# A four-layer gated cross-attention kernel: one batch's rows normalised ahead of the other's, and weight turns placed anew

## The reference, cut to what matters

```python
# second layer, feed-forward (quantised, with a Hadamard transform)
gate = bitlinear(x, w_gate); up = bitlinear(x, w_up)          # 256 -> 1024, rows rounded to 8 bits
intermediate = jax.nn.silu(gate) * up
return h_bitlinear(intermediate, w_down)                      # fwht over 1024, round to 8 bits, 1024 -> 256

# third layer: the attention branch is a mixing of rows with a learned adjacency
return (1.0 - gamma) * adj_raw + gamma * A_learned            # adj_raw is the normalised x
# third layer, feed-forward: a shared part and two of eight experts
g = x @ sw1.T; u = x @ sw2.T
shared_out = jax.nn.silu(g) * u @ sw3.T                       # 256 -> 1024 -> 256
scores = jax.nn.sigmoid(x @ router_w.T)
_, top_idx = jax.lax.top_k(scores + expert_bias, TOPK)
```

## Time and profile before

| what | value |
|---|---|
| median of 3 runs | 748.82 us (748.71 to 749.53) |
| profiled execution, its own time | 750.36 us |
| span of that execution | 748.5 us |
| PE busy | 663.1 us (89%) |
| DVE busy | 529.6 us (71%) |
| ACT busy | 350.4 us (47%) |
| POOL busy | 224.5 us (30%) |
| granted TensorE clock, mean | 0.972 |

### The profile page before, as it was taken

One profiled execution on the slowest core, in us unless ns is written; L12 is line 12 of the kernel. 1 busy time (PEld: TensorE's weight loads), 2 busy tenths in 40 slices (PEclk: granted clock), 3 DMA queues, 4 the chain that ended last, 5 costly groups with the idle time before them and its releaser, 6 DMA issues. The chain is left out here.

```text
span 748.5 us, 13940 instructions
## 1 busy us (share of the span) xinstructions
PE 663.1 (89%) x4446; PEld 455.1 (61%) x4446; DVE 529.6 (71%) x1617; ACT 350.4 (47%) x620; POOL 224.5 (30%) x315
## 2 busy tenths in 40 slices
PE   9998898898888887899789999976788989999997
PEld 4644476766764665487567778652233328777776
DVE  5686988879787788878875572757986967335545
ACT  2573456576455755142126326235488794122220
POOL 1000377812000122112315652632352220623430
PEclk9999999999999999999999999996799999999999
DMA  6997431050000230000071260012000053233315
GB/s 174 341 235 152 162 101 49 17 171 1 3 2 1 77 94 1 1 0 1 30 253 59 64 205 22 29 44 72 2 2 2 4 173 61 79 106 100 93 57 175
DMA packets 55565, 60.23 MB, mean 80 GB/s; under 512 B 13847, under 2 KB 48808, under 8 KB 55496
## 3 DMA queue, kind: packets, MB, share of 16 engines
q1 hardware_dynamic: 50408, 46.02, 21.8%
q0 software_dynamic: 4848, 13.28, 5.1%
q10 hardware_dynamic: 240, 0.05, 0.0%
HBM read 34.92 MB, written 24.20 MB: 79 GB/s over the span
## 5 line engine op out<-in xcount | busy, mean ns | idle before, releaser
L2068 ACT ACTIVATE arenas<-psum 128x512 f32<-128x512 f32 (+6 forms) x89 | 62.9, 733 | 47.9 <-PE psum L1215 40.0
L3356 DVE TENSOR_REDUCE arenas<-psum 128x2 f32<-128x512 f32 x96 | 61.8, 683 | 12.2 <-PE psum L1819 10.9
L1023 POOL TENSOR_SCALAR arenas<-arenas,small 128x1024 f32<-128x1024 f32 x8 | 9.0, 1124 | 151.3 <-DVE small L3047 151.3
L1040 POOL DMA_INDIRECT experts_l<-shared,small x30 | 29.5, 982 | 62.7 <-ACT shared L2381 51.7
L2068 ACT ACTIVATE late<-psum 128x512 f32<-128x512 f32 (+1 forms) x51 | 25.6, 503 | 43.1 <-PE psum L1215 43.0
L1215 PE MATMUL psum<-conb,shared 128*128 128x128 bf16 (+2 forms) x512 | 37.6, 229 | 7.2 <-issue 2.1
L1215 PEld LDWEIGHTS psum<-conb,shared 128*128 128x128 bf16 (+2 forms) x512 | 33.2, 118 | 14.6 <-issue 12.0
L1215 PE MATMUL psum<-con,early 128*128 128x128 f32 (+1 forms) x188 | 32.2, 282 | 10.7 <-ACT late L2068 5.1
L2428 ACT ACTIVATE early<-psum 128x1024 f32<-128x1024 f32 x32 | 32.0, 1031 | 17.1 <-PE psum L1836 16.7
L1703 PE MATMUL psum<-arenas,early 128*128 128x256 f32 x160 | 36.7, 383 | 1.1 <-DVE arenas L3510 1.1
L1703 PE MATMUL psum<-early,late 128*128 128x256 f32 x128 | 32.5, 403 | 5.4 <-DVE early L3249 5.3
(11 more groups left out here) (456 smaller groups left out, 1763.7 us busy)
## 6 DMA issues: line engine op xcount, KB each, us to landing
sorted_l<-late SPq DMA_DIRECT2D x3, 1920.0 KB, 17.4
early<-sorted_l SPq DMA_DIRECT2D x6, 645.0 KB, 5.8
early<-in_L_ffn_sw SPq DMA_DIRECT2D x3, 1024.0 KB, 9.7
late<-sorted_l SPq DMA_DIRECT2D x23, 129.0 KB, 2.1
sorted_l<-late SPq DMA_DIRECT2D x1, 2944.0 KB, 24.5
early<-in_L_ffn_We_gate_up SPq DMA_DIRECT2D x2, 1408.0 KB
early<-in_L_ffn_expert_w SPq DMA_DIRECT2D x2, 1024.0 KB, 6.8
early<-in_L_ffn_w SPq DMA_DIRECT2D x1, 2048.0 KB, 8.3
```

The lines of the kernel that those rows point to most:

```text
L1023: pool.tensor_scalar(ha[s][:, rows], ha[s][:, rows], c2[s][:, t:t + 1], ROUND, ALU.mult, ALU.add)
L1040: pool.indirect_dma_start(expert_rows2[p], bass.IndirectOffsetOnAxis(dest2[p][:, i:i + 1], 0), out_r2[k], None).then_inc(outs_sent[k], 16)
L2068: act.activation(dst, view(v), ACT.Copy, scale=scale).then_inc(f.drained(i, key), 1)
L3356: dve.tensor_reduce(nm, q3d(f.slot(0, ("max", w, k)), 2, S), X, ALU.max, negate=True)\
```

## The change

Four things are altered.

1. `beside_f1`: the same 25 turns of `prep2` stand at other steps. They stand one after the other, without gaps, from the turn of a product to the first parts of the transform, and none stands in the transform's third and fourth part.
2. `second_rows` in `ffn1`: statistics run ahead of the first multiplication, and the other seven parts behind the multiplications of the first two tiles instead of the first four.
3. `mix(0)` becomes `mix_first`: statistics and root of all four row tiles of the pair come first; batch 0's rows are written and signalled in the second step, before batch 1 is mixed; then batch 1 gets statistics and root anew and is written.
4. TensorE and ScalarE in `ffn2(0)`: eight constant matmuls, the turn of batch 0, the first two shared blocks of batch 0 (`AHEAD2`) with their silu, 14 constant matmuls, the turn of batch 1. Both turns now use bank 2, and the shared blocks keep banks 0 and 1.

```diff
--- before.py
+++ after.py
@@ -610,7 +610,9 @@
                         H=(h, 1, [("hT", i) for i in range(TILES2)]), D=(d, 1, [("dn", i) for i in range(TILES2)]))
 
         plan("l1f", 1, B=([4, 5], 1, products1(1)))
-        plan("l2f", 0, **ffn2_keys([0, 1], 2, [("AT", 0), ("AT", 1)]))
+        plan("l2f", 0, A=([2], 1, [("xT", 0), ("xT", 1), ("gate",), ("rank",)]),
+             B=([0, 1], 1, streams([("sh", j) for j in range(HC)]) + [("AT", 0), ("AT", 1)]), N=([2], 1, [("dn", 0), ("dn", 1)]))
+        AHEAD2 = 2
 
 
 
@@ -716,7 +718,7 @@
 
         THERE_F1 = 50
 
-        beside_f1 = paced(6, (22, 1.5)) + [41, 45, 48]
+        beside_f1 = [6, 7, 8, 9, 10, 11, 15, 16, 17, 18, 22, 23, 24, 25, 26, 27, 31, 32, 33, 34, 35, 36, 40, 41, 44]
 
         TILES_THERE = 9
 
@@ -1715,21 +1717,31 @@
 
                 fa, fb = pl["l2f"]["A"], pl["l2f"]["B"]
 
+                rows = (fa, fa if i == 0 else fb)
+
+                def shared2(s, j):
+                    shared_up(fb, i, s, j, xnT2[i], P, j * P, j * P, sw1T, sw2T, H_FFN)
+
                 if i == 0:
                     yield from steps(MIX)
-                if i == 0:
-                    kept_busy(fa, i, ("xT", 0), 34)
+                    kept_busy(fa, i, ("xT", 0), 8)
                 for s in range(2):
                     pe.wait_ge(xn_ready["l2f"].sem, xn_ready["l2f"].count(2 * i + s))
-                    turn((fa, fb)[s], i, ("xT", s), [(P, c * S + t * P, rows2[i][:, s * T + t, c * P:(c + 1) * P])
-                                                     for c in range(DC) for t in range(T)], ident)
+                    turn(rows[s], i, ("xT", s), [(P, c * S + t * P, rows2[i][:, s * T + t, c * P:(c + 1) * P])
+                                                 for c in range(DC) for t in range(T)], ident)
+                    if (i, s) == (0, 0):
+                        pe.wait_ge(fa.drained(0, ("xT", 0)), fa.read(0, ("xT", 0)))
+                        for j in range(AHEAD2):
+                            shared2(0, j)
+                        kept_busy(fa, i, ("xT", 1), 14)
                 yield
                 for s in range(2):
-                    pair_logits(fa, (fa, fb)[s], i, s, xnT2[i], r2T)
+                    pair_logits(fa, rows[s], i, s, xnT2[i], r2T)
                     yield
                 for s in range(2):
                     for j in range(HC):
-                        shared_up(fb, i, s, j, xnT2[i], P, j * P, j * P, sw1T, sw2T, H_FFN)
+                        if (i, s) != (0, 0) or j >= AHEAD2:
+                            shared2(s, j)
                         if (s, j) == RANK[i]:
                             pe.wait_ge(picks2_ready, i + 1)
                             rank(fa, i, 2 * T, picked2[i])
@@ -2338,10 +2350,19 @@
 
             def ffn2(i):
                 fa, fb = pl["l2f"]["A"], pl["l2f"]["B"]
+
+                def gate2(s, j):
+                    act.wait_ge(fb.filled, fb.full(i, ("sh", s, j)))
+                    v = fb.slot(i, ("sh", s, j))
+                    act.activation(sg2[i][fb.place(i, ("sh", s, j))], v[:, 0:S], ACT.Silu).then_inc(sg2_ready, 1)
+
                 if i == 0:
                     yield from steps(MIX)
                 for s in range(2):
-                    move((fa, fb)[s], i, ("xT", s), xnT2[i][s], lambda v: v[:, 0:W])
+                    move(fa if i == 0 else (fa, fb)[s], i, ("xT", s), xnT2[i][s], lambda v: v[:, 0:W])
+                    if (i, s) == (0, 0):
+                        for j in range(AHEAD2):
+                            gate2(0, j)
                 yield
                 yield
                 act.wait_ge(fa.filled, fa.full(i, ("gate",)))
@@ -2350,9 +2371,8 @@
                 yield
                 for s in range(2):
                     for j in range(HC):
-                        act.wait_ge(fb.filled, fb.full(i, ("sh", s, j)))
-                        v = fb.slot(i, ("sh", s, j))
-                        act.activation(sg2[i][fb.place(i, ("sh", s, j))], v[:, 0:S], ACT.Silu).then_inc(sg2_ready, 1)
+                        if (i, s) != (0, 0) or j >= AHEAD2:
+                            gate2(s, j)
                         yield
 
             def downs2(i):
@@ -3050,6 +3070,7 @@
 
                 alone(quantise(0))
                 second = second_rows()
+                advance(second, 1)
                 yield from steps(2)
                 for step in range(TILES1 + 3):
 
@@ -3065,7 +3086,10 @@
                             dve.wait_ge(fb.drained(part, ("g", i, s, t, h)), fb.read(part, ("g", i, s, t, h)))
                             dve.scalar_tensor_tensor(ha[s][:, at:at + BANK], v, up_scale[i][1][s][:, t:t + 1], sg1[2 * t + h],
                                                      ALU.mult, ALU.mult).then_inc(fb.drained(part, ("u", i, s, t, h)), 1)
-                            next(second, None)
+                            if step == 0:
+                                advance(second, 2)
+                            elif step == 1:
+                                advance(second, 1 + h)
                             yield
                     if 0 <= step - 1 < TILES1:
                         if step == 2 * T + 1:
@@ -3142,10 +3166,31 @@
                     last.then_inc(xn_ready["l2f"].sem, 1)
                     yield
 
-            def mix(i):
-
-                yield from mixed_steps(2 * i + 1)
-                norm_rows("l2f", i, rows2[i])
+            def mix_first():
+
+                def written(k, at, row):
+                    return normalised(k, rows2[0][:, at, 0:D], row)
+
+                rows, own = x_rows(range(1)), x_rows(range(1, 2))
+                dve.drain()
+                statistics(rows + own)
+                alone(root_steps(EPS))
+                yield
+                for t in range(T):
+                    last = written(t, t, rows[t])
+                last.then_inc(xn_ready["l2f"].sem, 1)
+                for t in range(T):
+                    normalised(T + t, bfly[:, t * D:(t + 1) * D], own[t])
+                dve.drain()
+                dve.scalar_tensor_tensor(xs[:, 1, :], bfly[:, 0:W], keep_x, xs[:, 1, :], ALU.mult, ALU.add)
+                dve.drain()
+                dve.scalar_tensor_tensor(xs[:, 1, :], adj[:, 1, :], keep_a, xs[:, 1, :], ALU.mult, ALU.add)
+                dve.drain()
+                yield
+                root_of_x(1, 1)
+                for t in range(T):
+                    last = written(t, T + t, own[t])
+                last.then_inc(xn_ready["l2f"].sem, 1)
                 yield
 
             def mixing(n):
@@ -3164,15 +3209,6 @@
                 dve.scalar_tensor_tensor(xs[:, n, :], adj[:, n, :], keep_a, xs[:, n, :], ALU.mult, ALU.add)
                 dve.drain()
                 yield
-
-            def mixed_steps(n):
-                parts = mixing(n)
-                for _ in range(5):
-                    next(parts)
-                yield
-                alone(parts)
-                yield
-
 
             def gated(sg, gate, tanh):
 
@@ -3251,7 +3287,7 @@
 
             def ffn2_first():
                 dve.wait_ge(pl["prep2b"]["A"].filled, pl["prep2b"]["A"].full(0, ("r",)))
-                yield from mix(0)
+                yield from mix_first()
                 yield from steps(3)
                 for s in range(2):
                     for j in range(HC):
```

## The result

The changed kernel takes 743.33 us (742.20 to 745.62, median of 4 runs) against 749.17 us of the kernel before in the same session: ratio 0.9895, 95% interval [0.9857, 0.9933]. In a later session it took 745.62 us against 751.92: 0.993 [0.9911, 0.9949]. One run of the kernel before in that session, 788.13 us at a mean clock of 0.854, was in a slower state and is left out of the ratio. The medians differ by 5.8 and 6.3 us and the ratios stand for 7.9 and 5.3 us, so the change makes the kernel faster by some 6 us; the forecast was 742.3 against 748.82, a ratio of 0.9913. The profiled execution has a span of 743.8 us, 4.7 less than before, at a mean clock of 0.968.

A forecast was written before the change was run, and what follows sets the result against it. VectorE and TensorE were taken to wait in turn in `ffn1`, with VectorE setting the pace afterwards. Gains of 4.3 us in `ffn1` and 2.2 in the head, 6.5 together, take 748.82 to 742.3 us; range 740.3 to 746.7.

The forecast's parts named there:

- transform 0: In `ffn1`, VectorE's transform: start at 252.6, 0.6 us later than before, behind a wait of 2.2 us for TensorE's product.
- transform 1: In `ffn1`: start at 259.8 against 264.00 before, with no VectorE wait, since no second-pair work stands between.
- transform 2: In `ffn1`: start at 269.7 against 273.00, after TensorE waits 1.3 us for GpSimd's tile 0; VectorE ready at 267.0.
- transform 3: In `ffn1`: start at 280.3 against 285.22, 4.9 us earlier by the chain; 4.3 us taken.
- The allowance from 4.9 to 4.3: In `ffn1`: gain put at 3.2 to 4.9 us, 4.3 taken, for semaphore gaps at hand-overs and time at lower clock.
- spell of low clock: In `ffn1`: a spell at 1.2 GHz falling on a product in the chain would cost 1.7 us.
- the load's landing: In `ffn1`: w12's load lands 8.3 us after turn 7, at 264.4; its turn comes at 264.0, the 0.4 already counted.
- the slack ahead of the routing: Third layer's head: logits end at 322.7, routing needs them at 325.2; 2.3 us of slack cover the 14 constant matmuls.
- Only the head gains: Rival: VectorE still waits for TensorE in `ffn1`, denser turns delaying products; only 2.2 us gained, 746.6 us; chance 0.11.
- Only `ffn1` gains: Rival: the head's 2.2 us wait reappears at the routing or a later block; 4.3 us gained, 744.5 us; chance 0.11.
- PE at 1.2 GHz in `ffn1`: Rival: TensorE slowed by its new wait for GpSimd; twenty us of it cost 12, 754 us; chance 0.06.
- Clock falling early in the head: Rival: clock falls while TensorE fills or turns in the third layer's head; routing waits 4.8 us, 747.1 us; chance 0.06.

The follow-up runs named there:

- e3: Kernel before with only the new places of the 25 weight turns in `ffn1`; 752.18 us, ratio 1.001 to the kernel before.
- e4: Kernel before with only the second pair's statistics, normalising and rounding moved ahead in `ffn1`; 751.43 us, ratio 1.0001 to the kernel before.
- e5: The changed kernel run once more, unaltered, in a later session; 745.62 us, ratio 0.993 to the kernel before.
- e1: Kernel before with both `ffn1` edits and the old head of the third layer; 747.48 us, ratio 0.9965 to the kernel before.
- e8: Changed kernel with 34 instead of 14 constant matmuls ahead of batch 1's turn; 747.63 us, ratio 0.9941 to the kernel before.
- e10: Changed kernel with 7 instead of 14 constant matmuls ahead of batch 1's turn; 755.20 us, ratio 0.9951 to the kernel before.
- e7: Changed kernel with no shared blocks ahead of batch 1's turn (`AHEAD2` 0 instead of 2); 748.81 us, ratio 0.996 to the kernel before.
- e2: Kernel before with only the new head of the third layer, both `ffn1` edits undone; 752.80 us, ratio 1.0011 to the kernel before.
- e6: Changed kernel with the 25 weight turns placed later on the whole; 742.38 us, ratio 0.9882 to the kernel before.
- e9: Changed kernel with turns as in e6, but the last ones spread over steps 37 to 46; 752.08 us, ratio 0.9911 to the kernel before.

## Why the prediction was right

**Step by step in `ffn1`.** The prediction's times, taken from 235.03, against the measured ones, taken from 236.22:

| step | predicted | measured |
|---|---|---|
| tile 2's first multiplication | 14.0 | 13.5 |
| transform 0 | 17.6, wait 2.2 | 17.8, wait 2.67 |
| transform 1 | 24.8, no wait | 24.9, no wait |
| TensorE gets GpSimd's tile 0 | 27.1, wait 1.3 | 27.9, wait 2.03 |
| transform 2 | 34.7, wait 2.7 | 36.0, wait 3.00 |
| transform 3 | 45.3 (4.9 us), 4.3 taken | 46.0 (4.20 us) |

The largest error in the chain is at transform 2, 1.3 us. 0.2 come from transform 0; GpSimd was 0.6 later than its 9.5 us behind it, because "the contention gone" was only half right: gone at the rounding, it came back elsewhere (below); and the transform started 2.5 us after its product instead of 2.1. Why it is more than at transform 0 is not explained, but it stands in the trace of the kernel before as well, where transform 2 starts 2.49 us behind its product; the prediction had read the distance at transform 0 alone:

```profile
270.51 2.02 PE L1667 MATMUL psum<-con,arenas 128*128 128x128 f32 x16 [0.39 <-ACT arenas L2068]
```

 Transform 3 got 0.6 back. The allowance from 4.9 to 4.3, written down for hand-overs and a spell of low clock, happened to have the size of these errors, which were mostly others; that the start of transform 3 came out to 0.1 us is luck. Two slips change no result: the load's landing was added up to 264.4 (255.5 and 8.3 are 263.8), and the slack ahead of the routing is 2.5 us by the prediction's own times, not 2.3. The load of w12 was issued at 257.08 (20.9 after the rounding; predicted 20.5) and took 8.4 us; it did not become a term.

**That it needed both edits** follows from the prediction's picture of two engines that wait in turn, but it was not said there, and the chances were given as if the edits were one. e3 and e4 show it.

**The spell of low clock.** The same code in `ffn1` came in three versions: transform 2 at 36.0 (after, e5), at 36.8 to 37.1 (e1, e8, e10) or at 35.4 (e7). Windows of 11 us around the weight turns ahead of it (length, busy PE, PEld, DVE, ACT, POOL, clock, DMA share, GB/s), in after, in e1 and in the kernel before:

```profile
258.00:269.00 11.00, 8.12 (x67) 6.36 (x67) 10.39 (x19) 7.22 (x14) 4.77 (x4) 1.00 0.76 241
```

```profile
257.00:268.00 11.00, 8.51 (x58) 6.24 (x57) 9.83 (x17) 6.50 (x12) 4.86 (x4) 0.84 0.77 236
```

```profile
256.83:267.83 11.00, 8.18 (x57) 6.20 (x56) 10.32 (x24) 6.29 (x11) 3.21 (x3) 0.84 0.68 201
```

Where the clock is lower, transform 2 is 0.9 to 1.1 us late, and the stage is that much behind from there on. The prediction priced a spell at 1.7. In e7 the clock was at 1.00 in the first 12 us after the rounding, where every other kernel had 0.86; its transform 0 is 1.7 us earlier than in after, and the later spell (0.84) took most of that back.

The kernel before has the spell too, and so has e2 (0.84). Like against like, the new order of `ffn1` is therefore worth 3.3 us at transform 3 (before against e1), and 0.9 of the 4.20 in the profile of after is a spell that this execution did not have. Whether the new order makes the spell rarer can't be said from two executions without it and four with it (e7 is the fourth). Adding these 0.9 to e1's gain of 3.47 at the stage end gives 4.3; with e2's 2.06 that is 6.4 of the 6.53 measured together. In the profiles the two parts add up; the times of the runs do not show it, since e2's show no gain.

**The head** went as predicted: batch 0's rows 72.2 us after the rounding (72.1 predicted, with the 4.3 taken off), batch 1's 78.7 (78.7), two blocks 77.3 (77.1), logits 83.5 (83.4), 2.2 to 2.4 us of slack (2.3, or 2.5 by its own times), the wait of 2.22 gone and none in its place. Counted from transform 3 to the first hidden, the stretch takes 39.05 us before, 40.12 with early rows and no block ahead (e7), and 36.8 with the blocks ahead (e2, after); a later turn of batch 1 costs nothing up to the slack and its full length beyond it (e8).

**The sum.** At the first hidden the gain is 6.49 us and at the stage end 6.53, predicted 6.5, so it was passed on whole through the stretch in which VectorE sets the pace. That the sum hit the profile to 0.1 us is partly luck, since it holds the 0.9 us of the spell; the path and the head's terms were right. By the medians of the runs 5.8 and 6.3 us are left. From the stage end to the end of the span the ten profiled executions ahead of the third session took 363.3 to 365.7 us with one code, and the rounding starts anywhere from 232.9 to 237.3; these scatters are over a third of the gain, and they blur the single parts (e2 above all). In the third session the stretch behind the stage end took 373, and the kernel before took 759 us there. Against e6, VectorE in e9 has lost 3.8 us by 440, in the third layer's experts, and 5.5 more between 637 and 664, where one wait for an expert's silu takes 11.05 us and not 6.88. What brings this about is open.

**The rivals.** "Only the head gains" is ruled out by e1, in time and profile; the waits of 2.67 and 3.00 us that spoke for it came, and so did the transform 1 without one that spoke against. "Only `ffn1` gains" would have a wait at the routing or a later block, and there is none beyond the 0.56 us at a later block that was there before. PE at 1.2 GHz in `ffn1`: the window of the seven tiles in the kernel after has a mean clock of 0.96 against 0.93 in the earlier trace rows, although TensorE has new waits of 2.0 and 3.0 us:

```profile
235.80:282.20 46.40, 39.96 (x299) 29.81 (x300) 36.45 (x85) 32.54 (x55) 10.16 (x9) 0.96 0.22 69
```

Clock falling early in the head: it fell at 320.9, behind the logits, as before. VectorE sets the pace there, so it cost nothing; windows of after and of e8 around the blocks behind the logits:

```profile
320.90:324.20 3.30, 3.30 (x10) 2.65 (x9) 3.00 (x8) 2.00 (x3) 2.02 (x2) 0.53 0.00 0
```

```profile
325.00:328.00 3.00, 3.00 (x17) 2.59 (x16) 2.39 (x17) 2.26 (x3) 0.57 (x1) 1.00 0.00 0
```

With 34 constants the clock stayed at 1.00 and the blocks took 3.67 us instead of 5.36, without any gain: what VectorE waited for was the logits. TensorE had no gap over 0.8 us in either kernel from 306 to the blocks, and yet the clock fell in one of them (0.53 from 320.9) and not in the other (1.00 from 325.0). The Trainium skill (TensorE: Matmul & The Clock Gate, Part 1, The HAM clock gate) has idleness bring the low rate back; here it came to a busy engine, behind transposes and products of 8 columns.

## What to carry to other kernels

Where two in-order engines wait for each other in turn, take away both waits in one edit before judging either: here each alone moved the end of the chain by 0.6 and 1.6 us, none of which could be seen in the time, and the pair moved it by 3.3 us. An engine that is filled with make-work until its data come should be given the part of its real work whose data can be had first, and the slack behind it measured by adding make-work until a wait appears. Side work through a single bank costs a wait for the copy (0.69 us here) whenever two turns follow each other directly, and next to nothing with other work of the same engine between them. Where it stands can still be improved after the first gain: e6's list was 3.2 us faster by the medians, of which the profile shows 1.4. Before a gain of a few us in one profile is put down to the change, look at whether the clock was the same in both executions: here one spell of low clock was worth 0.9 us.

## What the hardware showed besides

Time that VectorE and GpSimd cost each other is not in the list of waits; it shows as instructions that take longer. In the changed kernel VectorE's L3059 at 263.10 took 1.52 us instead of 0.68. GpSimd's timeline of the same kernel:

```profile
261.32 1.04 POOL L1028 TENSOR_SCALAR arenas<-arenas 128x1024 f32<-128x1024 f32 x1 [0.16 <-issue]
262.51 1.58 POOL L1030 TENSOR_SCALAR shared<-arenas 128x1024 bf16<-128x1024 f32 x1 [0.15 <-issue]
```

GpSimd's L1030 usually takes 1.04 and took 1.58. The times fit if the three ran one behind the other: VectorE's L3058 to 263.1, then GpSimd's 1.04 to 264.1, then L3059's 0.68 to 264.8, where the trace has 264.6. The Trainium skill (SBUF — State Buffer, Who interferes with whom) says that a VectorE instruction with two SBUF inputs contends with a GpSimd instruction that reads SBUF, and calls the ports that they share an exclusive lock. The trace agrees. It agrees on the other side too: L3050 and L3051 of transform 1, which read one of their inputs from PSUM, overlap L1028 (261.32 to 262.36) and took their usual 0.67 and 0.68 us. So in this trace GpSimd's rounding does not slow every VectorE instruction beside it; the pair that met lost 0.84 and 0.54 us.

The low clock behind the logits with TensorE busy throughout was known from the kernel before and stays unexplained. That a spell comes in some executions of one code and not in others around 22 to 33 us after the rounding was not expected; what brings it about is open.
